# Feed-forward products from rounded part and remainder, and paired score units, in a one-core transformer block

## The reference

```python
x = x + attn(layernorm(x))                 # 16 heads of 8, causal, sequence 512
h = layernorm(x)
for i in range(6):                         # 16 heads of 64, window 32, rotary
    h = local_attn(shift(h), Wqkv[i], qs[i], ks[i], Wo[i]) + h
    h = ffn(shift(h), g[i], bln[i], W1[i], b1[i], W2[i], b2[i]) + h
x = x + h

def ffn(x, g, bln, W1, b1, W2, b2):
    xn = layernorm(x) * g + bln
    a, gate = split(xn @ W1 + b1)          # 341 columns each
    return a * gelu(gate) @ W2 + b2
```

## Time and profile before

| | us |
|---|---|
| median of 3 runs | 4179.59 |
| lowest and highest | 4172.83, 4183.58 |
| profiled execution, its own time | 4182.92 |
| its span | 4181.1 |
| PE busy | 3900.5 (93%) |
| DVE busy | 3305.5 (79%) |
| ACT busy | 3091.6 (74%) |
| POOL busy | 2581.2 (62%) |
| mean granted TensorE clock | 0.986 of full |

### The profile page before, as it was taken

The page is one execution under the profiler, slowest core; times in us unless marked ns, Lnnn a source line. Parts: engine busy times, 40 slices in busy tenths (PEclk is TensorE's granted clock), DMA queues, the critical chain, the costliest instruction groups (busy, mean ns, idle before and its releaser), DMA issues.

```text
span 4181.1 us, 190344 instructions
## 1 busy us (share of the span) xinstructions
PE 3900.5 (93%) x78816; PEld 3039.7 (73%) x78816; DVE 3305.5 (79%) x5294; ACT 3091.6 (74%) x10376; POOL 2581.2 (62%) x2583
## 2 busy tenths in 40 slices
PE   6888885999998999989999989999899999899998
PEld 3555554888866888848888668888488887588884
DVE  6778874988866888938888668989489886698894
ACT  5877785888865888838888658888488886588883
POOL 4667765766645676627666456766377664566660
PEclk9999998999999999999999999999999999999999
DMA  1000001111111111111111111111111111111110
GB/s 35 2 2 2 2 2 53 47 45 45 46 56 38 45 47 45 44 50 44 49 44 46 58 36 47 44 49 42 53 44 47 47 44 61 35 45 46 47 43 26
DMA packets 100195, 167.40 MB, mean 40 GB/s; under 512 B 26224, under 2 KB 33648, under 8 KB 99056
## 3 DMA queue, kind: packets, MB, share of 16 engines
q1 hardware_dynamic: 99312, 154.89, 12.6%
HBM read 26.13 MB, written 2.10 MB: 7 GB/s over the span
## 4 chain that ended last, share of the span: by engine, by line
PE 69%; issue 9%; POOL 3%; DVE 1%; ACT 0%; DMA 0%; SPq 0%; POOLq 0%; DVEq 0%; ACTq 0%
PE s_bank L1177 13%; PE s_bank L1246 10%; PE s_bank L1259 9%; PE s_bank L1198 8%; PE s_bank L1157 5%; PE s_proj L1222 4%; PE s_proj L1223 4%; PE s_proj L1224 4%; PE s_bank L1209 2%; PE s_bank L1210 2%; PE s_bank L1211 2%; PE s_bank L1167 2%; PE s_bank L1140 1%; POOL s_rotated L802 1%; PE s_bank L1289 1%
## 5 line engine op out<-in xcount | busy, mean ns | idle before, releaser
L802 POOL TENSOR_TENSOR s_rotated<-s_rotated,s_by_sin 128x512 f32<-128x512 f32 x768 | 983.8, 1302 | 227.3 <-DVE s_by_sin L1087 225.2
L811 POOL TENSOR_TENSOR s_probs<-s_probs,s_rden 128x256 f32<-128x256 f32 x768 | 479.7, 641 | 729.8 <-DVE s_rden L1027 729.3
L901 ACT ACTIVATE s_probs<-s_bank,s_neg_max 128x64 f32<-128x64 f32 x3072 | 908.0, 310 | 5.7 <-DVE s_neg_max L1020 5.6
L783 DVE TENSOR_TENSOR s_qk<-s_rotated,s_inv_norm 128x1024 f32<-128x1024 f32 x384 | 743.8, 1937 | 11.5
L1082 DVE TENSOR_TENSOR s_rotated<-s_proj,s_cos 128x1024 f32<-128x1024 f32 x384 | 469.6, 1223 | 241.5 <-ACT s_sq L935 240.9
L901 ACT ACTIVATION_READ_ACCUMULATOR s_probs<-s_bank,s_neg_max 128x1 f32 x3072 | 636.1, 207 | 0.0
L891 ACT ACTIVATE s_probs_t<-s_bank 64x512 f32<-64x512 f32 x384 | 226.8, 591 | 524.8 <-PE s_bank L1157 524.8
L1177 PE MATMUL s_bank<-s_qk 32*32 32x64 f32 x49152 | 581.4, 223 | 26.3 <-issue 25.9
L1177 PEld LDWEIGHTS s_bank<-s_qk 32*32 32x32 f32 x49152 | 510.9, 103 | 115.4 <-issue 114.6
L213 POOL TENSOR_TENSOR s_probs<-s_probs,s_rden 128x384 f32<-128x384 f32 (+3 forms) x512 | 406.4, 802 | 206.1 <-DVE s_rden L406 202.2
L824 POOL TENSOR_TENSOR s_sq<-s_sq 128x512 f32<-128x512 f32 x384 | 490.2, 1277 | 65.5 <-ACT s_sq L935 59.8
(11 more groups left out here) (118 smaller groups left out, 8156.2 us busy)
## 6 DMA issues: line engine op xcount, KB each, us to landing
s_v<-s_v SPq DMA_DIRECT2D x384, 192.0 KB, 2.5
s_v<-s_v SPq DMA_DIRECT2D x384, 64.0 KB, 2.4
s_qk<-f_wqk SPq DMA_DIRECT2D x6, 1024.0 KB, 6.4
s_xs_raw<-u SPq DMA_DIRECT2D x48, 128.0 KB
s_xf<-u SPq DMA_DIRECT2D x48, 128.0 KB, 2.3
s_xs_raw<-u SPq DMA_DIRECT2D x48, 127.8 KB
s_xf<-u SPq DMA_DIRECT2D x48, 127.8 KB, 2.6
s_qk<-f_wv SPq DMA_DIRECT2D x6, 512.0 KB, 6.8
```

The lines of the kernel that those rows point to most:

```text
L783: return nc.vector.tensor_tensor(qk[:, quad % 2, :, :, at:at + TOKS], rotated[:, par, :, :, :], by, ALU.mult)
L802: nc.gpsimd.tensor_tensor(rotated[:, par, :, half, :], rotated[:, par, :, half, :], by_sin[:, :, 1 - half, :], (ALU.subtract, ALU.add)[half])\
L811: nc.gpsimd.tensor_tensor(part, part, by, ALU.mult).then_inc(S["probs_done"], 1)
L901: last = nc.scalar.activation(probs[:, par, h, b, :], score_bank[h][:, b * KEYS:(b + 1) * KEYS], ACT.Exp, scale=-1.0, bias=neg_max[:, par, ...
```

## The change

1. **Feed-forward operands.** `w1`, `w2`, the normed tokens `xa` and the hidden activations each get a rounded copy (`_high`, float32r, made by ACT) and a remainder (`_rest`). Each fp32 product becomes three one-pass products. The weights' remainders are made by POOL in steps (2, 1) and (2, 2) of the layer, the tokens' remainders by POOL (`rest_of_xa`), the hidden remainders by DVE.
2. **Tail.** The up product of chunk 0 of sequence 0 moves from p = 0 to p = 3, beside that of chunk 1. ACT and POOL split the tokens of sequences 0 and 1 at p = 2 and 3.
3. **POOL in the feed-forward part.** Remainders of sequences 2 and 3, then the eight table operations, then the remainders of 4 to 7, then the next layer's weights. The wait for `f_xa` is gone.
4. **ACT.** After gate 2 of each sequence it rounds the tokens of sequence s + 2. It rounds the next layer's first tokens after sequence 5. Its last layer is written out behind the loop.
5. **Stage 1.** Masks in float32r in place of bf16. PE does the scores of two units together in even slots, and the transposes of two units together (t - 5 and t - 4) in odd ones. The copies of transposes move from four to five units behind.

```diff
+COPY_LAG = TR_LAG + 1
-        ident_b = sb("s1_ident_b", [P, P], BF16)
+        ident_r = sb("s1_ident_r", [P, P], F32R)
-        causal_b = sb("s1_causal_b", [P, P], BF16)
+        causal_r = sb("s1_causal_r", [P, P], F32R)
-                of = behind(s, par, t, TR_LAG, first)
+                of = behind(s, par, t, COPY_LAG, first)
...
+                if t < UNITS and t % 2 == 0:
+                    scores(s, par, t, first)
+                    scores(s, par, t + 1, first)
+                if t % 2 == 1:
+                    for lag in (TR_LAG + 1, TR_LAG):
+                        of = behind(s, par, t, lag, first)
+                        if of:
+                            transposes(of, first)
...
+XS_FFN = 5
+W1_AT, W2_AT = (2, 1), (2, 2)
+XA_AT = {(NSEQ, 2): 0, (NSEQ, 3): 1}
...
@@ POOL
+            def rest_of_xa(s, f):
+                nc.gpsimd.tensor_tensor(xa_rest[:, s % 2, :], seq_of(xa, s), xa_high[:, s % 2, :].bitcast(F32),
+                                        ALU.subtract).then_inc(S["xa_rest"], 1)
...
-                    tables(l + 1)
-                    nc.gpsimd.tensor_copy(in_rows(w_high[:, :]), w_raw).then_inc(S["w_high"], 1)
-                    pool.wait_ge(S["w_high"], l + 2)
-                    pool.wait_ge(S["f_xa"], l * NSEQ + NSEQ)
-                    nc.gpsimd.tensor_tensor(in_rows(w_rest[:, :]), w_raw, ...
+                    for s in range(2, NSEQ):
+                        f = l * NSEQ + s
+                        pool.wait_ge(S["xa_high"], f + 1)
+                        rest_of_xa(s, f)
+                        if s == 3:
+                            tables(l + 1)
+                    next_weights(l)
             steps(depth - 1, step)
+            second_part(depth - 1)
@@ ACT, ffn_gate
+                def rounded(c):
+                    act.wait_ge(S["f_hid"], f * NC + (c + 1))
+                    nc.scalar.activation(hid_high[0:m, s % 2, c, :], gate[c][0:m, :], ACT.Copy)
...
+                gates(0)
+                for c in range(1, NC):
+                    gates(c)
+                    rounded(c - 1)
+                if s < NSEQ - 2:
+                    tokens_ffn_high(l, s + 2)
+                rounded(NC - 1)
@@ DVE, ffn_hidden
+                def rest(c):
+                    dve.wait_ge(S["f_hhigh"], f * NC + (c + 1))
+                    nc.vector.tensor_tensor(hid_rest[0:m, par, c, :], gate[c][0:m, :],
+                                            hid_high[0:m, par, c, :].bitcast(F32), ALU.subtract)
+                product(0)
+                for c in range(1, NC):
+                    product(c)
+                    rest(c - 1)
+                rest(NC - 1)
@@ PE
-                    last = nc.tensor.matmul(up_bank[c][i][0:m, :], w1[:, ...], seq_of(xa, s), start=True, stop=True)
+                    nc.tensor.matmul(to, w1_high[:, cols], xa_high[:, s % 2, :], start=True, stop=False)
+                    nc.tensor.matmul(to, w1_high[:, cols], xa_rest[:, s % 2, :], start=False, stop=False)
+                    last = nc.tensor.matmul(to, w1_rest[:, cols], xa_high[:, s % 2, :], start=False, stop=True)
...
-                    pe.wait_ge(S["f_hid"], f * NC + (c + 1))
+                    pe.wait_ge(S["f_hrest"], f * NC + (c + 1))
...
-                pe.wait_ge(S["f_xa"], f + 1)
+                pe.wait_ge(S["xa_rest"], f + 1)
```

More of the change, by code:

```diff
@@ new lines, in scores @@
+            def scores(s, par, t, first):
+                g, b, i = UNIT_LIST[t]
+                if b == 0 and i == 0:
+                    pe.wait_ge(S["diag_vector"], (s * GROUPS + (g + 1)) * len(DIAG_VECTOR))
+                    pe.wait_ge(S["diag_pool"], (s * GROUPS + (g + 1)) * len(DIAG_POOL))
+                    pe.wait_ge(S["k_split"], s * GROUPS + (g + 1))
+                n = P * (b + 1)
+                if not (first and t < 4):
+                    pe.wait_ge(S["exp_done"], s * UNITS + (t - 3))
+                nc.tensor.matmul(score_bank[t % 4][:, 0:n], q_diag[:, par, g * HPG + i, b * P:(b + 1) * P],
+                                 k_t[:, par, g, 0:n], start=True, stop=False, skip_group_check=True)
+                nc.tensor.matmul(score_bank[t % 4][:, n - P:n], ident_r[:, :], causal_r[:, :],
+                                 start=False, stop=True, skip_group_check=True).then_inc(S["score_done"], 1)
@@ new lines, in transposes @@
+            def transposes(of, first):
+                us, _, u = of
+                pe.wait_ge(S["probs_done"], us * UNITS + (u + 1))
+                if u >= 2:
+                    pe.wait_ge(pt(u - 2), pt_count(us, u - 2))
+                elif not (first and u >= 0):
+                    pe.wait_ge(pt(UNITS + u - 2), pt_count(us - 1, UNITS + u - 2))
+                for kb in range(UNIT_LIST[u][1] + 1):
+                    done = nc.tensor.transpose(tr_bank[u % 2][:, kb * P:(kb + 1) * P],
+                                               probs[:, u % N_PROBS, kb * P:(kb + 1) * P], ident[:, :])
+                done.then_inc(S["tr_done"], 1)
@@ L656, in build_stage2 @@
         xa = sb("s2_xa", [P, TOK])
[L657 to L659 removed]
+        gate = [gate_sb[:, c, :] for c in range(NC)]
         names = ("const_in consts cast zeroed attn_w ffn_w tables w_high w_rest xs_in xs_high xs_rest proj_done sq_done sqadd_done prod_done "
@@ L954, in step, with ffn_gate, gates, layer @@
                                          bias=ln_shift[:, 0:1]).then_inc(S["inv_done"], 1)
-            def ffn_gate(f):
-                for c, (_, m) in enumerate(CHUNKS):
+            def ffn_gate(l, s):
+                f = l * NSEQ + s
+                def gates(c):
+                    m = CHUNKS[c][1]
                     act.wait_ge(S["f_up"], f * NC + (c + 1))
+                    wait(act, S["f_hrest"], (f - 1) * NC + (c + 1) if s else 0)
                     nc.scalar.activation(gate[c][0:m, :], up_bank[c][1][0:m, :], ACT.Gelu,
                                          bias=vec[0:m, 2 + NC + c:3 + NC + c]).then_inc(S["f_gate"], 1)
+                def rounded(c):
+                    m = CHUNKS[c][1]
+                    act.wait_ge(S["f_hid"], f * NC + (c + 1))
+                    nc.scalar.activation(hid_high[0:m, s % 2, c, :], gate[c][0:m, :], ACT.Copy)\
+                      .then_inc(S["f_hhigh"], 1)
+                gates(0)
[5 more added lines that the diff above has]
+                rounded(NC - 1)
             act.wait_ge(S["attn_w"], 16 * N_ATTN_DMA)
             nc.scalar.activation(in_rows(w_high[:, :]), w_raw, ACT.Copy).then_inc(S["w_high"], 1)
-            with act.Fori(0, depth) as l:
+            tokens_high(0, 0)
+            def layer(l, last):
                 steps(l, step)
@@ L969, in _ @@
                 f = l * NSEQ + NSEQ - 1
-                ffn_gate(l * NSEQ)
-                ffn_gate(l * NSEQ + 1)
-                centred_square(f)
-                ffn_gate(l * NSEQ + 2)
-                inverse_std(f)
-                ffn_gate(l * NSEQ + 3)
-                for s in range(4, NSEQ):
-                    ffn_gate(l * NSEQ + s)
+                for s in range(NSEQ):
+                    ffn_gate(l, s)
+                    if s == 1:
+                        centred_square(f)
+                    if s == 2:
+                        inverse_std(f)
+                    if s == XS_FFN and not last:
+                        tokens_high(l + 1, 0)
+            if depth > 1:
+                with act.Fori(0, depth - 1) as l:
+                    layer(l, False)
+            layer(depth - 1, True)
         @block.vector
```

128 lines of the change are left out of this document (76 added, 52 removed).

## The result

The changed kernel takes **4210.93 us** (median of 4 runs, 4207.43 to 4215.38), the kernel before beside it 4176.21 (4 runs, 4172.61 to 4183.58): ratio **1.0081, 95% interval 1.0063 to 1.0100**. It is slower by 0.8%. That lies at the upper end of the range that was given (4142 to 4212) and 24 us above the forecast of 4187. The profiled execution took 4207.43 with a span of 4205.3, 24.2 more than the span before.

A forecast was written before the change was run, and what follows sets the result against it. PE bounds attention steps and feed-forward; in stage 1 four engines wait in turn. Feed-forward +12, tail -1, splits +3, stage 1 -6 give +8 on 4182.9, 4191; the median lies 3.3 lower: 4187 us, range 4142 to 4212.

The forecast's parts named there:

- third rival, "stage 1 loses": Stage 1: transposes before the output product wait for later copies, masks cost more; 20 us slower, 4213 us, chance 0.18.
- Stage 1, "Bounds -30 to +20; I take -6": Stage 1: dearer masks, less ACT waiting for transposes, more PE waiting for copies; -6 us taken in all.
- The later copies take away ACT's waiting for transposes: Stage 1: copies one unit later remove ACT's waits for transposes, 33.5 us in 480; 45 us as upper bound.
- The product, 0.705 for three one-pass products: Feed-forward part: three one-pass products take 0.705 us in place of 0.859 for one fp32 product.
- First wait: Layers 0 to 4: PE waits before sequence 4 for POOL's remainder behind the tables, 6.2 us (3.9 to 7.5).
- Second wait: Layers 0 to 4: POOL's long remainder of the next weights holds a DVE remainder until 51.9, delaying the last down products.
- does not hold DVE: Feed-forward rival: POOL's long operation does not hold DVE for its length; 4159 us, chance 0.22.
- Layers 0 to 4, +4.3 each: Feed-forward parts of layers 0 to 4: 1.8 us longer by the chain plus 2.5 for the clock, each.
- The clock: Feed-forward parts: PE's waits bring stretches at nearly the lower clock level, 2.5 us a layer (0 to 4).
- Last layer, -9.4: Last layer's feed-forward part, without tables or next weights: 50.1 us against 59.5, a gain of 9.4.
- Tail and splits: Tail: moved up product, -1 us in all; attention steps: weights' splits nearly hidden, +3 us in all.
- Stage 1 should end near 675 us: Sign to check in the trace: stage 1 ends near 675 us; an end before 660 would refute the forecast.

The follow-up runs named there:

- two-piece: Changed kernel with stage 1 as in the kernel before, POOL's remainder of the next weights cut in two operations of 1536 columns: 4175.94 us, ratio 1.0001.
- six-piece: Changed kernel with stage 1 as in the kernel before, POOL's remainder of the next weights cut in six operations of 512 columns: 4166.91 us, ratio 0.9963.
- s1_old: Changed kernel with all of stage 1 as in the kernel before: 4188.63 us, ratio 1.0017.

## Why the prediction was right or wrong

The total was right to 0.6% and inside the range, in part by luck. Stage 1 was 36 us above its term; the feed-forward parts (12 below theirs) and the attention steps (11 below, for no cause in the change) took most of that back. The forecast's own range (4172 to 4202) missed, and "slower" had a chance of 0.31; the time is that of the third rival, "stage 1 loses", 4213 at a chance of 0.18.

- **Stage 1, "Bounds -30 to +20; I take -6": wrong in sign, +30.4.** This is the step that failed. The prediction prices masks and copies and gives the pairing of transposes no price at all, though the order excerpt ahead of it showed it. The runs put the whole loss there (1.0107 with it alone, 0.9986 with pairs of scores). The upper bound was 10 us short.
- **The rival "stage 1 loses" was right in its time and in its first half.** PE's waits for ACT's copies grew, 22.8 to 67.6 us. But the place was wrong: they are spread over the sequence, at a dozen or so of its 32 pairs. In the slot of the output product PE stands 0.70 us a sequence, 4.2 of those 67.6. Its other half, 1.5 us a sequence for dearer masks, is nil (1.0020 against 1.0017).
- **"The later copies take away ACT's waiting for transposes" was half right.** ACT's wait shrank with copies five behind, from 33.5 to 17.1 us, and PE's grew by more. With copies four behind, the same kernel has it the other way round, at the same time.
- **The product, 0.705 for three one-pass products: right.** The products stand 0.23 to 0.24 apart; six up products in threes take 4.31 us from the first to the down product behind them, forecast 4.23.
- **First wait: right in mechanism, 1.3 too long.** Tables' transfer at t = 14.2 (14.7 forecast), remainder of sequence 4 begun at 23.8, PE idle 4.88 us (6.2, between 3.9 and 7.5). But that wait is not what its removal brings back, as the expectations of the experiments had it: without the tables, PE waits at t = 20.8 for another engine, till 22.2.
- **Second wait: right.** POOL's remainder of the weights begins at t = 44.2 (45.2 forecast) and ends at 51.3 (51.9). A DVE remainder is held for 6.5 us, and the addition of sequence 5 is done at 54.3 (54.1). The two-piece and six-piece kernels confirm that the hold is taken for most of the operation's length. The rival "does not hold DVE" is refuted.
- **Layers 0 to 4, +4.3 each: mis-sized, +1.3 each.** In layers 0, 2 and 4 the last one-pass product of the part starts at t = 62.6 to 63.7, as the chain and the clock said (61.3 + 2.5); in layers 1 and 3 at 59.6 and 59.7, since there the last nine products stand 0.24 us apart and not 0.43 as at the lower clock. And the next layer's first product follows by 0.9 us where it followed by 2.3 (layer 0; 1.2 to 1.4 less in each of the five), so that part of the delay is not passed on. Both were left out of the forecast.
- **The clock: right in kind.** In the earlier trace rows this part had 1.00; now a stretch of layer 0 has 0.77 after the first wait, and two have 0.50 and 0.59 after the second.
- **Last layer, -9.4: mis-sized, -5.9.** 1.4 us at sequence 4, which waits for the gates behind ACT's three table loads, that I had not looked at; and the last product's stretch at a clock of 0.53, that I had given to layers 0 to 4 only. That stretch does not come in every trace: seven others with the same feed-forward code have 64.3 us for 65.84, a gain of 7.5.
- **Tail and splits:** +1.4 and nothing that can be told from the spread of the attention steps; forecast -1 and +3.
- **"Stage 1 should end near 675 us": wrong.** Its last work ends at 713.6 us, where it ended at 681.7 before. The test beside it looked to one side only ("before 660"); an end after 700 should have stood there too.

## What to carry to other kernels

Before steps in a ring of engines are grouped, count the buffers between them, and ask which unit of the group comes later than its reader wants it. Pairs of transposes over two banks cost 0.9% by themselves, and with paired scores the kernel was as slow with copies four units behind as with five; pairs of scores over four banks gained 0.2 to 0.3%. Where every engine is busy less in the same stretch, look for waits that grew, not for work that did. An expected time that comes true does not show the expected wait: look for the wait in the trace as well. When an operation is moved out of one wait's way, look whose way it is in now. A long POOL operation with two inputs in on-chip memory should be cut where DVE has such operations to do; six pieces cost POOL 2.5 us and gave the kernel 4 us a layer, because the price was paid on an engine with time to spare and the gain fell on the path.

## What the runs showed of the hardware

- DVE's two-input subtraction took 6.5 us beside one POOL operation of 7.14 us, 3.2 to 4.0 beside two of 3.8 to 3.9, at most 1.8 beside six, against a median of 0.69, while DVE operations that read PSUM and one SBUF tile kept 0.75 us beside the same operations.
- With the mask of 128 columns in float32r the kernel is no slower than with bf16 (ratios 1.0020 and 1.0017).
- In the changed kernel's first feed-forward part the granted clock of whole stretches was 0.50 to 0.77 behind PE waits of 4.2 and 4.9 us, where the kernel before, with PE busy 58.48 of 59.4 us, had 1.00. Nine products of 512 columns stood 0.43 us apart at the lower level and 0.24 at the upper. At the kernel's end a wait of 1.63 us was followed by the lower level in one trace (0.53) and by the upper in another (`s1_old`, the same wait, products 0.23 us apart).
